# A tile's gate and up products alternate between their two PSUM banks

## What is computed

```python
t = _layer_norm(h, ln2_g, ln2_b).reshape(-1, H)
logits = jnp.einsum('th,eh->te', t, gate_w)
top_vals, top_idx = jax.lax.top_k(logits, TOP_K)
...
for e in range(NUM_EXPERTS):
    g = jnp.einsum('th,ih->ti', t, gate_proj[e])
    u = jnp.einsum('th,ih->ti', t, up_proj[e])
    oe = jnp.einsum('ti,hi->th', jax.nn.silu(g) * u, down_proj[e])
    out = out + comb[:, e:e + 1] * oe
```

## Time and profile before

| | us |
|---|---|
| median of three runs | 365.0 (364.2 to 366.27) |
| the profiled execution, its time | 363.73 |
| the profiled execution, its span | 361.8 |
| TensorE busy with products in the span | 314.5 (87%) |
| VectorE busy | 256.4 (71%) |
| ScalarE busy | 239.0 (66%) |
| GpSimd busy | 201.8 (56%) |

### The profile page before, as it was taken

One profiled execution on the slowest core, in us unless ns is written; L12 is line 12 of the kernel. 1 busy time (PEld: TensorE's weight loads), 2 busy tenths in 40 slices (PEclk: granted clock), 3 DMA queues, 4 the chain that ended last, 5 costly groups with the idle time before them and its releaser, 6 DMA issues.

```text
span 361.8 us, 8735 instructions
## 1 busy us (share of the span) xinstructions
PE 314.5 (87%) x2052; PEld 271.0 (75%) x2052; DVE 256.4 (71%) x1039; ACT 239.0 (66%) x559; POOL 201.8 (56%) x243
## 2 busy tenths in 40 slices
PE   4878697668899989998999899899999999984970
PEld 3767487446789878887888788688888888873860
DVE  3468969789698869886987988767666766630660
ACT  2679656536867677686768677677777777750471
POOL 0245378857467655773786687686444433342760
PEclk9989989959999999999999999999999999996996
DMA  7178821133212121112112212332211111005931
GB/s 260 54 238 255 287 76 39 46 80 123 55 45 83 40 62 52 46 39 55 52 56 54 67 47 69 89 96 65 63 50 46 36 45 39 15 14 188 334 119 58
DMA packets 27872, 31.97 MB, mean 88 GB/s; under 512 B 4769, under 2 KB 21413, under 8 KB 27824
## 3 DMA queue, kind: packets, MB, share of 16 engines
q1 hardware_dynamic: 23504, 22.88, 21.1%
q0 software_dynamic: 4320, 8.53, 7.2%
HBM read 20.16 MB, written 11.68 MB: 88 GB/s over the span
## 4 chain that ended last, share of the span: by engine, by line
PE 68%; DVE 11%; issue 6%; ACT 5%; POOL 4%; DMA 3%; POOLq 0%; ACTq 0%; SPq 0%; DVEq 0%
PE bank L548 17%; PE bank L496 9%; PE bank L498 8%; PE bank L497 8%; PE bank L534 8%; PE bank L433 3%; PE bank L449 2%; PE bank L703 2%; PE bank L558 2%; POOL expert_rows L1360 2%; PE bank L697 2%; PE bank L473 2%; PE bank L410 1%; DVE hid L1203 1%; ACT xs L748 1%
## 5 line engine op out<-in xcount | busy, mean ns | idle before, releaser
L1369 POOL DMA_INDIRECT moe_rows<-ysb,xrow x71 | 70.4, 992 | 87.2 <-ACT ysb L774 80.7
L548 PE MATMUL bank<-wd,hidT 128*128 x568 | 76.4, 277 | 4.6 <-ACT t L781 3.9
L1360 POOL DMA_INDIRECT expert_rows<-rows,place x64 | 63.0, 985 | 23.7 <-issue 13.4
L548 PEld LDWEIGHTS bank<-wd,hidT 128*128 128x128 f32 x568 | 68.9, 192 | 7.3 <-issue 7.2
L496 PE MATMUL bank<-w_hi,t_hi 128*128 x142 | 63.3, 446 | 6.1 <-DVE hid L1203 4.0
L498 PE MATMUL bank<-w_hi,t_lo 128*128 x142 | 56.7, 399 | 0.0
L497 PE MATMUL bank<-w_lo,t_hi 128*128 x142 | 56.3, 397 | 0.0
L787 ACT ACTIVATE th<-bank 128x512 f32<-128x512 f32 x71 | 42.6, 600 | 15.4 <-PE bank L498 15.2
L1203 DVE SCALAR_TENSOR_TENSOR hid<-th,bank 128x512 f32<-128x512 f32 x71 | 48.3, 681 | 3.2 <-ACT th L787 3.2
L1207 DVE TENSOR_TENSOR hid<-hid,bank 128x512 f32<-128x512 f32 x71 | 48.8, 687 | 2.4
L800 ACT ACTIVATE hidT<-bank 128x512 f32<-128x512 f32 x71 | 42.6, 599 | 10.5 <-PE bank L534 10.2
(11 more groups left out here) (159 smaller groups left out, 570.4 us busy)
## 6 DMA issues: line engine op xcount, KB each, us to landing
xrow<-expert_rows SPq DMA_DIRECT2D x71, 66.0 KB, 1.9
w_raw<-weights SPq DMA_DIRECT2D x16, 256.0 KB, 4.1
w_lo<-moe_rows SPq DMA_DIRECT2D x16, 256.0 KB, 5.4
xT<-xt SPq DMA_DIRECT2D x8, 256.0 KB, 4.9
wd<-weights SPq DMA_DIRECT2D x4, 512.0 KB, 8.9
out<-xs SPq DMA_DIRECT2D x16, 128.0 KB, 1.7
xs<-x SPq DMA_DIRECT2D x3, 512.0 KB, 4.9
moe_rows<-ysb,xrow POOLq DMA_INDIRECT x71, 2.3
```

The lines of the kernel that those rows point to most:

```text
L548: last = mm(ps_y, hidT[i % 2][:, c * P:(c + 1) * P], wd[:, bass.ds(w + c * P, P)], start=(c == 0), stop=(c == NC - 1))
L1360: G.indirect_dma_start(out=expert_rows[:, :], out_offset=bass.IndirectOffsetOnAxis(ap=place[:, i, k:k + 1], axis=0), in_=rows[:, i, k, :], ...
L1369: G.indirect_dma_start(out=moe_rows[:, :], out_offset=bass.IndirectOffsetOnAxis(ap=xrow[i % XR][:, C_DST:C_DST + 1].bitcast(I32), axis=0), ...
```

## The change

The three gate products and the three up products of a tile are issued in turn, gate and up by product. Gate's last product is the fifth of the six and up's last the sixth, and each still raises its own semaphore. Both waits, for `ga_done` and for `hid_done` of the tile `two_ago`, now stand ahead of the first product. The operands, the count of products, the banks and the order of the sum within each bank are as before.

```diff
-            def gate_up(w, j, bank, i2):
-
-                mm(bank[:, :], t_hi[i2][:, :], w_hi[:, j, w], start=True, stop=False)
-                mm(bank[:, :], t_hi[i2][:, :], w_lo[:, j, w], start=False, stop=False)
-                return mm(bank[:, :], t_lo[i2][:, :], w_hi[:, j, w], start=False, stop=True)
+
+            def gate_up(w, gate, up, i2):
+                mm(gate[:, :], t_hi[i2][:, :], w_hi[:, 0, w], start=True, stop=False)
+                mm(up[:, :], t_hi[i2][:, :], w_hi[:, 1, w], start=True, stop=False)
+                mm(gate[:, :], t_hi[i2][:, :], w_lo[:, 0, w], start=False, stop=False)
+                mm(up[:, :], t_hi[i2][:, :], w_lo[:, 1, w], start=False, stop=False)
+                mm(gate[:, :], t_lo[i2][:, :], w_hi[:, 0, w], start=False, stop=True).then_inc(sm["g_ps"], 1)
+                mm(up[:, :], t_lo[i2][:, :], w_hi[:, 1, w], start=False, stop=True).then_inc(sm["u_ps"], 1)
...
                     two_ago = i - 2 if i >= FREE + 2 else i - 1
                     if two_ago >= 0:
                         pe.wait_ge(sm["ga_done"], two_ago + 1)
-                    gate_up(bass.ds(w_gate, INTER), 0, ps_g(i), i % 2).then_inc(sm["g_ps"], 1)
-                    if two_ago >= 0:
                         pe.wait_ge(sm["hid_done"], two_ago + 1)
-                    gate_up(bass.ds(w_gate, INTER), 1, ps_u(i), i % 2).then_inc(sm["u_ps"], 1)
+                    gate_up(bass.ds(w_gate, INTER), ps_g(i), ps_u(i), i % 2)
```

## The result

The changed kernel takes 388.26 us (387.03 to 389.55) against 365.16 us: a ratio of 1.063, interval 1.058 to 1.068. The forecast was 388, slower. The profiled execution of the changed kernel took 389.55 us with a span of 387.7, which is 25.9 more than the span of before (361.8). The medians lie 23.1 us apart; the profiled execution of before was 1.4 us quicker than its median, that of the changed kernel 1.3 us longer than its own. So differences between the two traces come out somewhat larger than the change is worth.

A forecast was written before the change was run, and what follows sets the result against it. TensorE was taken as the bound nearly throughout, with a 3.75 us loop setting minimum gaps up to tile 49. Added 23.4 us on the profiled 363.7 gave 387.1; the median's 1.3 made 388.4, stated as 388, range 379 to 395.

The forecast's parts named there:

- The ring: Up to tile 49, gate products, Tanh, two `hid` operations and release form a loop; no gap shorter than 3.75 us.
- rival 4: The new order doesn't arrive: three gate products still run first, both waits ahead; loop 3.29 us, 378 us; chance 0.02.
- the 0.9 that the prediction gave as a sign: Between tiles 28 and 49, TensorE idles about 0.9 us per gap ahead of the first gate product.
- The sum: Added time over gaps between tiles' gate starts plus the tail: 23.4 us, with ends 20.6 and 27.6.
- the floor: Lower sum, from short gaps growing to 3.75 us, tile 0 and the tail: 20.6 us, 14.5 in tiles 28 to 49.
- ring stage: Tiles up to 49, where gate and up have single banks and each tile waits for the one before.
- term (e): After the last tile's gate start nothing covers the later Tanh and `hid`: 0.46 us more.
- What costs nothing: From tile 50 banks alternate, so the wait and Tanh's 0.46 us delay add no time; product time unchanged at 0.23.
- ScalarE's cover: From tile 50, ScalarE's 0.61 us idle per tile absorbs Tanh's 0.46 us delay, leaving 0.15.
- Quick release: First gate product follows `hid` after 0.05 us, loop 3.53 us; 14 to 16 us more, 380 us; chance 0.13.
- Lower clock: TensorE's clock falls in one gap of ten up to tile 49: 5 us more, 393; chance 0.14, shared with the ceiling.
- Not slower: Repeated stationary `t_hi` skips TensorE loads; products shrink from 0.23 to 0.175 us or less, 365 us or faster; chance 0.04.

The follow-up runs named there:

- the wait alone: Against the kernel before: old order of gate then up products kept, both waits moved ahead of the first product; 376.89 us, ratio 1.034.
- gate last: Against the kernel before: up's three products first, then gate's three, both waits ahead; 397.83 us, ratio 1.087.
- the plan was first split: Kernel before with waits carried by the products, plus VectorE's plan of the next tiles (`plan_tiles`) cut in two over consecutive steps; 369.24 us, ratio 1.011.
- the last kernel: Kernel before with waits carried by the products and VectorE's `plan_tiles` split for its last two groups alone; 362.58 us, ratio 0.993.

## Why the prediction was right

**The ring.** 3.75 us forecast, 3.74 to 3.75 in the trace, term by term: Tanh 1.44 after the gate start (1.45 to 1.47 measured), `hid`'s end at 3.48 (3.50 to 3.51), the release 0.27 (0.24). The kernels that await `hid_done` ahead of the tile's first or second product lie in the order of their rings: 3.28, 3.40, 3.55, 3.75 and 3.98 us, with 73.5, 74.2, 77.2, 80.9 and 85.2 us for the stretch from tile 28 to 49, about 17 us for each us of ring. It isn't 21, one for each gap, since some gaps have another cause. The price of rival 4, a ring of 3.29 and 378 us, is close to what the wait alone turned out to have (3.28, 376.9). TensorE idles 0.65 ahead of a gate product and not the 0.9 that the prediction gave as a sign: the last row of a step, the transpose of token rows, lasts 0.27, and in the kernel before it overlapped the next gate product.

**The sum.** The prediction's rule for the 23.4 (each gap at least 3.75 and each `hid` end awaited), applied to the gaps of the trace before, gives 1.6 for tile 0, 1.4 for tiles 1 to 6, 3.1 for 6 to 22, 1.7 for 22 to 28 and 15.1 for 28 to 49. Measured were 1.6, 2.5, 2.9, 2.0 and 14.6. Of the 2.5, 1.1 is the clock in tile 1, below, which leaves the 1.4 forecast. Of the 2.8 above the floor 2.3 came, nearly all of it ahead of tile 28; between 28 and 49 the floor of 14.5 alone would have been nearer. The ring stage together is 23.55 us longer, where 22.9 was forecast.

**The tail**, term (e): from the last gate start to the transposes of `hid` 3.53 us (343.40 to 346.93) against 3.07 in the earlier trace rows, 0.46 as forecast. The other 0.7 of the 1.1 us comes after it, in the last stage, and has no instruction of the change in it.

**What costs nothing.** Right for time: 2.83 a gap from tile 50 on, and the run with the alternation there alone equals the kernel before. The step by which ScalarE's cover was reckoned was too narrow: 0.15 us was to be left, and the changed kernel has 0.25 ahead of `ysb`; gate last, at 0.7 us later, still fits. Products cost 0.23 from start to start in either order, as the earlier trace rows had it.

**The rivals.** Quick release: its physics was wrong for the changed kernel, and right for the kernel with the wait on the product, whose 381.7 is close to its 380. Lower clock: in the trace it happened in one gap, and there as the end of the lower clock of tile 0 and not as a fall; from tile 2 to tile 70 the clock stayed at 1.00. Not slower: no sign of a saved load, since the page after has 2052 loads for 2052 products, as the page before has.

**Errors that met.** The median of 388.26 is nearer to the forecast than the working deserves. In the ring the release was put 0.03 too long and `hid`'s end 0.02 to 0.03 too early, and the two cancel. In the ring stage the sum left out tile 1's clock (1.1 in this trace) and was 0.45 too high for the rest (22.9 against 22.45). From tile 49 to 70, put at nothing, the trace is 0.4 shorter, and the last stage 0.7 longer than the term for the tail.

## What to carry to other kernels

When an accumulation's bank is single, count the ring: from the first product, to the last product of the group that is consumed first, through its consumers, to the wait. Put each wait as late in the queue as its bank allows, and finish first the group that the longest chain waits for; alternating two groups delays the first and joins the waits of both. Work on another engine can be moved only into steps where a trace shows room; here the next step was full in four of the five places where the plan was first split (gaps 7, 15, 23 and 31).

## What the runs showed of the hardware

**From the end of `hid` to the product that waits for it.** For a product whose address comes from a register this took 0.24 us when the wait stood ahead of the instruction that forms the address, 0.14 when another product of the tile had gone ahead, and 0.05 when the product itself carried the wait. In the ring this was worth 6.6 us, in the kernel before nothing that can be told from noise. Which of the instructions between takes the time was not tried.

**The clock at the start of the ring.** In the kernel before TensorE's granted clock was 0.52 of full speed in tile 0 (the lower level, 1.2 GHz) and 1.00 from tile 1 on the earlier trace rows. After, it was 0.50 in tile 0 and 0.70 in tile 1, whose six products ran at the lower level too. The rows are the first two of them and Tanh:

```profile
85.84 0.79 PE L496 MATMUL bank<-w_hi,t_hi 128*128 x1 [1.68 <-DVE hid L1208]
86.43 0.63 PE L497 MATMUL bank<-w_hi,t_hi 128*128 x1
...
88.37 0.60 ACT L788 ACTIVATE th<-bank 128x512 f32<-128x512 f32 x1 [3.49 <-PE bank L500]
```

The later steps are 0.43 where the ring's are 0.23, and the gap is 4.81 where 3.75 was forecast. It is tempting to blame the 1.68 us that TensorE idled for `hid` ahead of tile 1, but the other runs don't bear this out. The kernel with the wait alone idled there too, for 0.82, and had 1.00 in tile 1. The kernel before with its waits on the products had 0.56 in tile 1, with TensorE busy throughout (columns as in the earlier trace rows):

```profile
83.08:86.32 3.24, 3.24 (x13) 2.55 (x12) 3.14 (x14) 1.43 (x3) 1.44 (x3) 0.56 0.65 209
```

And the kernel that alternates up to tile 49, with the same order up to there as the changed one, had the lower clock into tile 2 (0.53, a gap of 5.04). So the tile in which the clock rises differs between executions of nearly the same code, and the 1.1 us are not shown to come from the change. What sets it stays open; in a ring, a tile at the lower clock makes its gap longer by 1.06 us.

**Gaps of 2.83 or 2.85.** From tile 50 on some kernels take 2.83 us a tile and others 2.85, in the old order as well as in the alternating one (the last kernel has the old order and 2.83). What makes the difference, 0.4 us in all, stays open.
